# k's rotary products moved between the reciprocals, moment transfers of tile 3 re-dealt, FFN weight splits one job earlier

## The reference, cut to what matters

```python
h = shift_token(x)                        # second half of the width from the token before
q, k, v = split(h @ wqkv, 3)              # 8 heads of 64
q = l2norm(q) * qs;  k = l2norm(k) * ksc
q, k = rotary_xpos(q, k)                  # t*cos*scale + rotate_half(t)*sin*scale
o = local_attention(q, k, v)              # window 128: a tile looks at itself and the tile before
x = x + o @ wo
h = layernorm(shift_token(x)) * lg + lb   # mean and variance over 256
a, g = split(h @ w1 + b1, 2)
x = x + (a * gelu(g)) @ w2 + b2
```

## Time and profile before

| what | value |
|---|---|
| median of 3 runs | 2815.29 us (2814.48 to 2815.41) |
| the profiled execution, its own time | 2823.89 us |
| its span, first to last instruction | 2822.1 us |
| TensorE clock granted, mean | 0.988 |
| busy: TensorE, VectorE, ScalarE, GpSimd | 95%, 76%, 62%, 56% of the span |
| tile 0, 1, 2, 3 with the FFN, of most slabs | 14.7, 14.8, 16.4, 33.8 us |

### The profile page before, as it was taken

One profiled execution on the slowest core, in us unless ns is written; L12 is line 12 of the kernel. 1 busy time (PEld: TensorE's weight loads), 2 busy tenths in 40 slices (PEclk: granted clock), 3 DMA queues, 4 the chain that ended last, 5 costly groups with the idle time before them and its releaser, 6 DMA issues.

```text
span 2822.1 us, 66713 instructions
## 1 busy us (share of the span) xinstructions
PE 2690.0 (95%) x23280; PEld 2319.4 (82%) x23280; DVE 2146.8 (76%) x6398; ACT 1757.2 (62%) x4748; POOL 1577.9 (56%) x1758
## 2 busy tenths in 40 slices
PE   7999999999999999998999999999999999999998
PEld 6888888888888888887776788888888888888887
DVE  7788888877777877776655887777777778877875
ACT  4666666666666665665454666666666666666664
POOL 4565666556555665654212566655556566656554
PEclk8999999999999999999999999999999999999999
DMA  3121011002000000004100000000003000000000
GB/s 113 31 76 58 24 51 53 20 24 104 13 2 2 2 2 24 2 2 163 58 17 31 2 2 2 2 2 2 2 2 109 32 2 17 17 17 17 17 16 24
DMA packets 75899, 81.33 MB, mean 29 GB/s; under 512 B 37552, under 2 KB 61872, under 8 KB 74416
## 3 DMA queue, kind: packets, MB, share of 16 engines
q1 hardware_dynamic: 69792, 75.51, 8.1%
q10 hardware_dynamic: 5776, 1.56, 0.2%
HBM read 49.53 MB, written 26.74 MB: 27 GB/s over the span
## 4 chain that ended last, share of the span: by engine, by line
PE 52%; DVE 19%; ACT 12%; issue 8%; POOL 7%; ACTq 2%; DMA 1%; DVEq 0%; POOLq 0%
PE bank L1018 9%; PE bank L1020 8%; PE bank L1019 8%; ACT pr L767 7%; PE bank L1219 5%; PE bank L1108 4%; PE bank L1078 4%; PE bank L1094 3%; PE bank L1054 3%; DVE t L1523 3%; DVE t L1520 3%; PE bank L1363 2%; POOL pr L607 2%; DVE pr L1550 2%; DVE h L1611 2%
## 5 line engine op out<-in xcount | busy, mean ns | idle before, releaser
L607 POOL TENSOR_TENSOR pr<-pr,rden 128x512 f32<-128x512 f32 (+1 forms) x512 | 467.6, 940 | 516.6 <-DVE rden L1559 512.7
L767 ACT ACTIVATE pr<-pr,nb 128x256 f32<-128x256 f32 (+1 forms) x1024 | 479.5, 470 | 276.5 <-DVE nb L1550 273.4
L1550 DVE CUSTOM_DVE_ANT_0 pr<-bank,maskb,r 128x256 f32<-128x256 f32 (+1 forms) x1024 | 401.8, 447 | 26.8 <-PE bank L1078 17.6
L1018 PE MATMUL bank<-h2T,w 128*128 128x256 f32 x1408 | 406.8, 289 | 12.9 <-DVE h2T L1577 12.9
L1019 PE MATMUL bank<-h2T,w 128*128 128x256 f32 x1408 | 395.9, 281 | 0.0
L1020 PE MATMUL bank<-h2T,w 128*128 128x256 f32 x1408 | 395.7, 281 | 0.0
L634 POOL TENSOR_TENSOR uTl<-t,uTh 128x256 fp32r<-128x256 f32 x320 | 238.1, 748 | 277.3 <-ACT uTh L842 277.3
L1625 DVE SCALAR_TENSOR_TENSOR t<-bank,b,t 128x256 f32<-128x256 f32 (+1 forms) x384 | 181.8, 480 | 215.5 <-ACT t L830 102.2
L1018 PE MATMUL bank<-wqkv,hT 128*128 128x512 f32 x768 | 306.2, 399 | 8.5 <-DVE nb L1550 5.7
L1019 PE MATMUL bank<-wqkv,hT 128*128 128x512 f32 x768 | 305.5, 398 | 0.0
L1020 PE MATMUL bank<-wqkv,hT 128*128 128x512 f32 x768 | 302.5, 394 | 0.0
(11 more groups left out here) (229 smaller groups left out, 6978.3 us busy)
## 6 DMA issues: line engine op xcount, KB each, us to landing
wqkv<-wqkv_split SPq DMA_DIRECT2D x18, 512.0 KB, 6.2
w<-w_split SPq DMA_DIRECT2D x3, 2816.0 KB, 9.9
Y<-in_x SPq DMA_DIRECT2D x8, 512.0 KB, 8.2
out<-Y SPq DMA_DIRECT2D x8, 512.0 KB, 3.5
stt<-stt SPq DMA_DIRECT2D x224, 3.0 KB
h<-out SPq DMA_DIRECT2D x7, 512.0 KB, 3.9
out<-h SPq DMA_DIRECT2D x7, 512.0 KB, 2.9
wqkv_split<-wqkv SPq DMA_DIRECT2D x1, 3072.0 KB, 11.7
```

The lines of the kernel that those rows point to most:

```text
L607: e.tensor_tensor(pr[:, 2 * j:2 * j + 2, 0:wide], pr[:, 2 * j:2 * j + 2, 0:wide], rden[:, 2 * j:2 * j + 2].unsqueeze(2).to_broadcast([P, 2 ...
L767: last = e.activation(pr[:, hd, 0:wide], pr[:, hd, 0:wide], ACT.Exp, bias=nb[:, hd:hd + 1], scale=-1.0, accum_out=den[:, hd:hd + 1])
L1018: e.matmul(out, left[0], right[0], start=first, stop=False)
L1550: m = e.tensor_tensor_reduce(pr[:, hd, 0:wide], bank[j][:, g * 256:g * 256 + wide], far, r[:, t, 1, place(hd):place(hd) + 1], FAR, ALU.add ...
```

## The change: what it does

- `K_part` 0, 1 and 2 are k's two rotary products and their sum. VectorE now runs one of them after each of the reciprocals R of pairs 1, 2 and 3, ahead of the sum of k's squares. ScalarE's squares of k wait for `rotk` (both products made) in place of `k_ps`.
- Tile 3's moments: SyncE's queue carries the long transfer that ScalarE's carried; ScalarE's keeps that of one row.
- `U_rest` comes ahead of `LN_moments(L, b, 1)` on VectorE, and GpSimd's `LN(L, b, 1)` comes behind `U_lo` of job 1.
- The w2 splits stand one job earlier on both engines.
- In b = 4 of L = 0 and 1 SyncE waits for the moments' transfers before it stores w2.

```diff
--- before.py
+++ after.py
@@ -359,10 +359,8 @@
         def out_buffer(b):
             return h[:, :, :] if b < B - 1 else cut(flat(t1[:, :, :], 0, NT * D), NT)
 
-        def move_first_halves(e, t, q):
-            e.dma_start(stt[0:P - 1, t + 1, 12:18], stt[1:P, t, 0:6]).then_inc(q, 16)
-            if t:
-                e.dma_start(stt[P - 1:P, t, 12:18], stt[0:1, t, 0:6]).then_inc(q, 16)
+        def move_first_row(e, t, q):
+            e.dma_start(stt[P - 1:P, t, 12:18], stt[0:1, t, 0:6]).then_inc(q, 16)
 
         def give_credits(e, share):
 
@@ -378,8 +376,9 @@
 
                 e.wait_ge(st_done, at(st_done, idx(L, b, t) + 1))
                 e.dma_start(stt[1:P, t, 6:12], stt[0:P - 1, t + 1, 18:24]).then_inc(q, 16)
-                if t < 3:
-                    move_first_halves(e, t, q)
+                e.dma_start(stt[0:P - 1, t + 1, 12:18], stt[1:P, t, 0:6]).then_inc(q, 16)
+                if 0 < t < 3:
+                    move_first_row(e, t, q)
                 if t in (0, 2):
                     e.dma_start(stt[0:1, t + 1, 6:12], stt[P - 1:P, t + 1, 18:24]).then_inc(q, 16)
                 if t == 2:
@@ -546,6 +545,7 @@
                 if L == 0:
                     store_layer0(b)
                 if L < DEPTH and b == 4:
+                    stats_moved(L, b)
                     store_w2(L)
                 if L == DEPTH - 1 and last:
                     mid_entry(L, b)
@@ -644,10 +644,11 @@
                         A1(*ahead, (L, b, 0) if t == 2 else None)
                     if L == 0 and t == 0 and b < B - 1:
                         entry_rstd(b + 1)
-                LN(L, b, 1)
                 for half in range(2):
                     for i in range(1, MT):
                         U_lo(L, b, half, i)
+                        if (half, i) == (0, 1):
+                            LN(L, b, 1)
                         if L == DEPTH and b == 0 and half and i in (3, 5):
                             out_rstd(B // 2 - 1, i // 3 - (i == 3))
 
@@ -738,7 +739,7 @@
 
             def A1(L, b, t):
                 m = idx(L, b, t)
-                e.wait_ge(k_ps, at(k_ps, m + 1))
+                e.wait_ge(rotk, at(rotk, m + 1))
                 e.wait_ge(ssk_done, at(ssk_done, m))
                 e.activation(sq[:, 0, :], bank[0][:, :], ACT.Square).then_inc(sqk, 1)
                 e.wait_ge(q_ps, at(q_ps, m + 1))
@@ -866,7 +867,7 @@
                     next_hi(i)
                 table(ACT.Gelu)
                 e.wait_ge(st_done, at(st_done, idx(L, b, 3) + 1))
-                move_first_halves(e, 3, st_moved[1])
+                move_first_row(e, 3, st_moved[1])
                 for mt in range(MT):
                     G(L, b, 0, mt)
                     if mt:
@@ -876,8 +877,8 @@
                 for mt in range(MT):
                     G(L, b, 1, mt)
                     U_hi(L, b, MT + mt - 1)
-                    if L < DEPTH and b == 0 and 1 <= mt <= 3:
-                        split_w2_hi(L, mt - 1)
+                    if L < DEPTH and b == 0 and mt < 3:
+                        split_w2_hi(L, mt)
                     if mt == 0:
                         for i in next_pieces(L, b)[1:2]:
                             next_hi(i)
@@ -1497,36 +1498,54 @@
 
             def A1(L, b, t, LN_of=None):
                 m = idx(L, b, t)
-                if L and b == 0 and t == 0:
-                    e.wait_ge(rot_loaded, at(rot_loaded, 16 * L))
-                if m == 0:
-                    e.wait_ge(rot_scaled, at(rot_scaled, 2))
-                if L == 0 and b and t == 1:
-                    e.wait_ge(nx_stored, at(nx_stored, 16 * 2 * b))
-                if t == 1:
-                    e.wait_ge(u_hi, at(u_hi, 12 * (8 * L + b)))
-                    e.wait_ge(u_lo, at(u_lo, 10 * (8 * L + b)))
-
-                def heads(ap):
-                    return ap.rearrange("p (h c j) -> p h c j", h=HEADS, c=2)
-
-                for i, (squared, rotated, added, sums, summed, read) in enumerate((
-                        (sqk, rotk, kr_step, ssk, ssk_done, guard_k), (sqq, rotq, qrot, ssq, ssq_done, guard_q))):
-                    f = 2 * (1 - i)
-                    e.wait_ge(squared, at(squared, m + 1))
-                    e.wait_ge(read, at(read, m))
-                    e.tensor_reduce(sums[:, :], sq[:, i, :].rearrange("p (h d) -> p h d", h=HEADS), AX.X, ALU.add).then_inc(summed, 1)
-                    e.wait_ge((kt_ps, qt_ps)[i], at((kt_ps, qt_ps)[i], m))
-                    e.tensor_tensor(t1[:, i, :].rearrange("p (h d) -> p h d", h=HEADS),
-                                    bank[i][:, :].rearrange("p (h d) -> p h d", h=HEADS),
-                                    rot[:, t, f:f + 1, :].to_broadcast([P, HEADS, DH]), ALU.mult)
-                    e.tensor_tensor(heads(t2[:, i, :]), heads(bank[i][:, :])[:, :, ::-1, :],
-                                    rot[:, t, f + 1:f + 2, :].to_broadcast([P, HEADS, DH]).rearrange("p h (c j) -> p h c j", c=2),
-                                    ALU.mult).then_inc(rotated, 1)
-                    e.wait_ge(rotated, at(rotated, m + 1))
-                    e.tensor_tensor((kr, qr)[i], t1[:, i, :], t2[:, i, :], ALU.add).then_inc(added, 1)
-                    if LN_of and i == 0:
-                        LN_moments(*LN_of)
+                K_sums(m)
+                if LN_of:
+                    LN_moments(*LN_of)
+                e.wait_ge(sqq, at(sqq, m + 1))
+                e.wait_ge(guard_q, at(guard_q, m))
+                e.tensor_reduce(ssq[:, :], sq[:, 1, :].rearrange("p (h d) -> p h d", h=HEADS), AX.X, ALU.add).then_inc(ssq_done, 1)
+                e.wait_ge(qt_ps, at(qt_ps, m))
+                rotary(1, t, 0, 0)
+                rotary(1, t, 0, 1).then_inc(rotq, 1)
+                e.wait_ge(rotq, at(rotq, m + 1))
+                e.tensor_tensor(qr, qr, t2[:, 1, :], ALU.add).then_inc(qrot, 1)
+
+            def rotary(i, t, f, part):
+
+                if part == 0:
+                    return e.tensor_tensor(t1[:, i, :].rearrange("p (h d) -> p h d", h=HEADS),
+                                           bank[i][:, :].rearrange("p (h d) -> p h d", h=HEADS),
+                                           rot[:, t, f:f + 1, :].to_broadcast([P, HEADS, DH]), ALU.mult)
+                halves_of = [ap.rearrange("p (h c j) -> p h c j", h=HEADS, c=2) for ap in (t2[:, i, :], bank[i][:, :])]
+                return e.tensor_tensor(halves_of[0], halves_of[1][:, :, ::-1, :],
+                                       rot[:, t, f + 1:f + 2, :].to_broadcast([P, HEADS, DH]).rearrange("p h (c j) -> p h c j", c=2), ALU.mult)
+
+            def K_part(L, b, t, part):
+
+                m = idx(L, b, t)
+                if part == 0:
+                    if L and b == 0 and t == 0:
+                        e.wait_ge(rot_loaded, at(rot_loaded, 16 * L))
+                    if m == 0:
+                        e.wait_ge(rot_scaled, at(rot_scaled, 2))
+                    if L == 0 and b and t == 1:
+                        e.wait_ge(nx_stored, at(nx_stored, 16 * 2 * b))
+                    if t == 1:
+                        e.wait_ge(u_hi, at(u_hi, 12 * (8 * L + b)))
+                        e.wait_ge(u_lo, at(u_lo, 10 * (8 * L + b)))
+                    e.wait_ge(k_ps, at(k_ps, m + 1))
+                    e.wait_ge(kt_ps, at(kt_ps, m))
+                    rotary(0, t, 2, 0)
+                elif part == 1:
+                    rotary(0, t, 2, 1).then_inc(rotk, 1)
+                else:
+                    e.wait_ge(rotk, at(rotk, m + 1))
+                    e.tensor_tensor(kr, kr, t2[:, 0, :], ALU.add).then_inc(kr_step, 1)
+
+            def K_sums(m):
+                e.wait_ge(sqk, at(sqk, m + 1))
+                e.wait_ge(guard_k, at(guard_k, m))
+                e.tensor_reduce(ssk[:, :], sq[:, 0, :].rearrange("p (h d) -> p h d", h=HEADS), AX.X, ALU.add).then_inc(ssk_done, 1)
 
             def A2(L, b, t):
                 m = idx(L, b, t)
@@ -1721,6 +1740,8 @@
                     S(L, b, t, 3)
                     for j in range(1, 4):
                         R(L, b, t, j)
+                        if ahead:
+                            K_part(*ahead, j - 1)
                         if L == 0 and b < B - 1 and j < 3:
                             if t == 0:
                                 entry_stats(b + 1, j)
@@ -1752,8 +1773,8 @@
                 for mt in range(MT):
                     U(L, b, 0, mt)
                     if mt == 1:
+                        U_rest(L, b, 0)
                         LN_moments(L, b, 1)
-                        U_rest(L, b, 0)
                     if mt == 2:
                         LN_apply(L, b, 1)
                     if mt == 4:
@@ -1762,8 +1783,8 @@
                     U(L, b, 1, mt)
                     if mt == 1:
                         U_rest(L, b, 1)
-                    if L < DEPTH and b == 0 and mt > 2:
-                        split_w2_lo(L, mt - 3)
```

(4 more changed lines are left out.)

## The result

The changed kernel takes 2863.13 us (median of 4 runs, 2860.98 to 2866.37) against 2815.35 for the kernel before in the same comparison (4 runs): a ratio of 1.0168, 95% interval 1.0150 to 1.0185. That is 48 us slower. The forecast was 2869, 54 us slower.

What follows compares the result with a forecast made beforehand. TensorE, busy 95%, was taken as the bound, waiting on three chains, two through GpSimd. 32 x (0.85 + 0.50) + 30 x 0.54 + 5 - 10 = +54 on the median gave 2869 us, range 2808 to 2906.

Steps and rivals of the forecast that it cites:

- K's addition holds GpSimd: Behind pair 3's reciprocal, k's two-SBUF-input addition waits for the third NP; the fourth NP then ends 0.54 us late.
- Tile 2: Late NP and a second collision at L594 delay LN and LN_apply, so WO comes 0.85 us later a slab.
- the hairline case of the prediction: Tile 2: q's addition goes ahead of L594 by 0.1 us; if L594 came first, the cost would be about 0.4.
- Tile 3: L594, and with it k's transposes and all behind them, come 0.54 us later in 30 slabs.
- The second price: Tile 3: ScalarE's squares wait for both k products, delaying v and the pT copies; said to lie beside the 0.54.
- Tile 0: K comes later and q sooner; taken as 0, with bounds 0 to 0.5 us.
- L = 0: Next sequence's layernorm pieces between the reciprocals bring up to three more 0.54 collisions in seven slabs: 5 us, bounds 0 to 11.
- FFN: LN waits for U_lo of job 1, starting 0.93 us later; LN_apply saves 0.43: net +0.50 a slab, bounds 0.4 and 0.93.
- One-offs: Earlier w2 split saves 3.3 us twice, the store behind the moments' transfers 3 to 4: together -10.
- The clock falls: Rival: longer TensorE waits in tile 2 and the FFN lower the granted clock, adding 20 us: 2889; chance 0.13.
- The chain is untouched: Rival: k's addition slips between GpSimd passes without holding the next; +1.5 us, 2817; chance 0.12.
- The early gelus win: Rival: in the FFN U_hi of job 1 moves up with gelu 0 and 1, LN not late: -28 us, 2787; chance 0.14.

Runs made afterwards that it cites:

- extra_two_inputs: Kernel before plus an unused VectorE addition of 128x512 with two SBUF inputs behind the last reciprocal of tiles 1 and 2: 2859.95 us.
- addition_behind_q_sum: Changed kernel with k's addition two places later on VectorE, behind q's sum of squares: 2846.66 us, ratio 1.0098.
- both_moved: Changed kernel with k's addition behind q's sum of squares and q's addition waiting for the end of k's product L594: 2846.67 us, ratio 1.0099.
- best_of_both: Kernel before plus one-offs and two moments queues, k's products early only in tiles 1 and 3 from L = 1 on: 2791.96 us, ratio 0.9906.
- one_offs_only: Kernel before with only the earlier w2 split and SyncE's w2 store behind the moments' transfers: 2810.70 us, ratio 0.9972.
- rotary_only: Kernel before with only K_part between the reciprocals and ScalarE's squares of k waiting for rotk: 2870.09 us, ratio 1.0186.
- extra_one_input: Kernel before plus two unused VectorE operations of one SBUF input behind the last reciprocal of tiles 1 and 2: 3020.22 us.

## Why the prediction was right, step by step

**K's addition holds GpSimd**: right, with the sizes 0.45 for 0.54. The addition does end 0.55 behind the third NP, but the next pass is only 0.45 longer, not 0.54: I took the addition's remainder for the hold. The added operation of extra_two_inputs shows both figures again.

**Tile 2**, 0.85 forecast: 0.80. The order at L594 was the hairline case of the prediction, decided by 0.1 us. It fell as taken, by 0.04: q's addition at 1764.91, L594 at 1764.95. addition_behind_q_sum and both_moved take the two holds away one after the other, and tile 2 goes from +0.80 to +0.3 to -0.2. The sign given, a wait of WO of 1.7, came as two: 0.61 for k's transposes (0.27 in the other slabs) and then 1.22.

**Tile 3**, 0.54 forecast: 0.43. The mechanism was right. The second price was named too, as beside the first: the squares' delay "lies beside the 0.54". What the traces add is its size, 0.36 on the way to the transposes of Y. With these at 11.54, k's transposes can't start before 11.94, against 12.11 in the changed kernel, so that freeing the NP alone would give back some 0.2 of the 0.43 at most; no run frees it alone.

**Tile 1**, 0: right from L = 1 on. **Tile 0**, 0 forecast with bounds 0 to 0.5: wrong in sign, -0.28 to -0.34 in 21 of the 24 slabs from L = 1 on. The first three of L = 2 change by +0.9, -0.1 and +0.1, so it makes 5.4 us without the one-offs. The step that failed is "TensorE reaches q's transposes behind k's, and these wait for GpSimd; I take no gain". TensorE in tile 0 of another slab of the kernel before with its window, and GpSimd, VectorE and TensorE of the changed kernel:

```profile
1858.03:1872.15 14.12, 13.71 (x107) 11.04 (x106) 10.80 (x34) 10.50 (x32) 10.30 (x14) 1.00 0.00 1
...
1869.67 0.65 PE L1054 MATMUL bank<-ident,t 128*128 128x128 f32 x4 [0.28 <-DVE t L1527]
```

```profile
1895.95 1.20 POOL L594 TENSOR_TENSOR t<-t,r 128x512 f32<-128x512 f32 x1
...
1895.55 0.69 DVE L1511 TENSOR_TENSOR t<-t 128x512 f32<-128x512 f32 x1
...
1897.20 0.66 PE L1055 MATMUL bank<-ident,t 128*128 128x128 f32 x4 [0.49 <-POOL t L594]
...
1897.94 0.60 PE L1055 MATMUL bank<-ident,t 128*128 128x128 f32 x4
```

Before, q's transposes waited for q's addition, and O stood behind it on VectorE. Now k's transposes start 10.91 behind the tile's start instead of 10.47. Tile 0 has both holds too: the fourth NP takes 1.05 in place of 0.61, but the guard behind it waits for k's sum in any case, which starts 0.28 later; and L594, 0.28 late by that, takes 1.20 in place of 1.04, since q's addition is issued 0.40 ahead of it. Q's start at 11.65 in both, but follow without a wait, and WO comes at 12.01 where it came at 12.34: q's addition, which now ends at 9.95 instead of 11.59, no longer stands in the way of q's transposes and of O. How much of the gain comes from the moved waits (see best_of_both) is open. The slab that I had read, doesn't show it: its tile 0 takes 14.66, the usual one 14.12.

**L = 0**, 5 us forecast with bounds 0 to 11: some 9 us beyond what its slabs share with the others, and not by more collisions. VectorE and GpSimd in tile 2 of L = 0, b = 3 of the changed kernel:

```profile
319.69 0.67 DVE L1520 TENSOR_TENSOR t<-bank,rot 128x512 f32<-128x512 f32 x1
320.28 0.76 DVE L1689 TENSOR_SCALAR Y<-Y,mv,rs 128x256 f32<-128x256 f32 x1
320.96 0.15 DVE L1578 RECIPROCAL rden<-den 128x2 f32<-128x2 f32 x1
...
321.19 1.41 POOL L607 TENSOR_TENSOR pr<-pr,rden 128x512 f32<-128x512 f32 x1 [0.30 <-DVE rden L1578]
```

A product and a piece of the next sequence's layernorm now stand ahead of the reciprocal, and the third and fourth NP each wait 0.30 for it. So the four NP end 9.0 behind the tile's start and not 8.1, and tile 2 loses 1.4 here.

**FFN**, 0.50 forecast with bounds 0.4 and 0.93: 0.25, under both. Two of its terms were right: `LN` starts 0.91 later (0.93 forecast) and `LN_apply` saves 0.45 (0.43). The term that was mis-sized is `LN` itself. I kept its 1.40, though `U_rest`, whose two SBUF inputs had held it, was moved away in the same change; by my own rule it had to fall, and it fell to 1.17: 0.91 - 0.45 - 0.23 = +0.23. The experiments show that this is a sum of parts that no one had to take together: the two queues give 0.27, `U_rest` ahead of the moments costs 0.23 of it, and `LN` behind `U_lo` costs 0.27.

**One-offs**, -10: -8.5 by one_offs_only; in the changed kernel's own slabs tile 0 of b = 1 is shorter by 3.2 in L = 0 and 3.8 in L = 1 and the FFN of b = 4 in L = 1 by 4.3, 11.3 in all.

**The sum.** With the measured terms it is 32 x (0.80 + 0.25) + 30 x 0.43 - 5.4 + 9.3 + 1.6 - 11.3 = +40.7, where the 1.6 are a tile 2 with a fallen clock (below), and the two spans are 39.7 apart. The 1.0 between is itself a balance: 1.4 more at the start and 0.9 more in the stretch with the memory layer, against single stretches in which the kernel before was longer, such as the last slab's tile 3 (17.29 against 15.99, at a mean clock of 0.80 against 0.89). The forecast of 54.4 was 13.7 over the sum: 8.0 in the FFN, 5.4 in tile 0, 4.9 in tiles 2 and 3 and 1.3 in the one-offs, against 5.9 too little in L = 0 and for the clock. That misses of both signs met is luck. Against the medians the forecast is only 6 over, because the profiled execution of before was 8.6 slower than its median. I had added the sum to the median, and that the result came so near is partly this. How much of the 8.6 belongs to windows of a fallen clock in that one execution, such as the last of the earlier trace rows, I didn't separate.

**The rivals.** *The clock falls*: hardly in the changed kernel. Its mean is 0.992, its runs lie within 5.4 us, and of its tiles 2 one is touched, that of L = 0, b = 4, 1.6 us longer than its neighbours:

```profile
396.13:415.50 19.37, 17.32 (x138) 15.09 (x137) 15.74 (x51) 9.90 (x29) 11.59 (x11) 0.91 0.01 2
```

But rotary_only shows it in six tiles of one execution, and extra_one_input in tile 2 of every slab, behind a wait of 1.52. It was a real risk: rotary_only shows it behind waits of 0.61 and 1.22, which the changed kernel has too. *The chain is untouched*: out by both added-work kernels. *The early gelus win*: half right. With `LN` and `U_rest` in their old places the earlier gelus are worth 0.27 a slab; the new order gave it away.

## What to carry to other kernels

An idle gap on VectorE is no free place if GpSimd runs an unbroken chain at that time: ask of each operation put there whether it has two SBUF inputs, or is a tensor_scalar from SBUF to SBUF (both kinds held GpSimd here), and what GpSimd has queued behind. The price is not the wait of the moved operation but that of the pass behind it, and of whatever moves into the next pass in its turn: here one move made two collisions in tiles 0 and 2. Read more than one slab before a tile is called free; and when an order is changed, test its parts one by one, since here the one-offs and the two queues, worth -18 us alone, were hidden behind the rotary part, worth about +50, and the new order of `LN` and `U_rest`, 0.50 a slab or some 16 us.

## What the runs showed of the hardware

A 128x512 addition of two SBUF inputs, issued inside a GpSimd pass, takes 1.16 us (1.38 in tile 3, where it is issued earlier in the pass) in place of 0.69 and ends 0.55 behind that pass; the next pass of an unbroken chain takes 1.49 in place of 1.04, a guard of 128x8 0.68 in place of 0.24, a power of 128x4 1.46 in place of 1.01. Beside the power of 128x8 an addition that was issued behind it (0.68) and the power (1.66) are as long as alone; issued 0.3 us ahead of the power, it makes that 1.93. But for the addition behind that power, which isn't held though GpSimd is at work, the order of issue decides who waits. The Trainium skill, SBUF — State Buffer, "Who interferes with whom", has it so, and these traces agree but for that one.

A tensor_scalar of 128x512 with one SBUF input is held too (0.91 and 1.15, each ending 0.28 behind the pass), which I had not expected, and holds the pass behind it by 0.19.
